# A decoder on one core: lane 7 of the batch-axis attention laid by GpSimd and lane 6 by ScalarE, where DMAs brought both

## The reference

```python
def split_heads(x):
    return x.reshape(L, N, h, d).transpose(1, 2, 0, 3)
q = split_heads(query @ q_proj.T + q_bias) * scale
k = split_heads(query @ k_proj.T + k_bias)
v = split_heads(query @ v_proj.T + v_bias)
scores = jnp.einsum('nhld,nhkd->nhlk', q, k)
scores = jnp.where(causal, scores, jnp.float32(-10000.0))
attn = jax.nn.softmax(scores, axis=-1)
ctx = jnp.einsum('nhlk,nhkd->nhld', attn, v)
ctx = ctx.transpose(2, 0, 1, 3).reshape(L, N, h * d)
return ctx @ out_proj.T + out_bias
```

## Time and profile before

| | us |
|---|---|
| median of 3 executions | 1265.68 |
| lowest, highest | 1263.89, 1273.03 |
| the profiled execution | 1265.68 |
| its span in the profile | 1263.9 |
| PE busy (share of the span) | 1133.7 (90%) |
| DVE busy | 908.6 (72%) |
| ACT busy | 565.4 (45%) |
| POOL busy | 261.0 (21%) |

### The profile page before, as it was taken

The page is one execution under the profiler, slowest core; times in us unless marked ns, Lnnn a source line. Parts: engine busy times, 40 slices in busy tenths (PEclk is TensorE's granted clock), DMA queues, the critical chain, the costliest instruction groups (busy, mean ns, idle before and its releaser), DMA issues. The chain is left out here.

```text
span 1263.9 us, 23937 instructions
## 1 busy us (share of the span) xinstructions
PE 1133.7 (90%) x8865; PEld 728.0 (58%) x8880; DVE 908.6 (72%) x2118; ACT 565.4 (45%) x1513; POOL 261.0 (21%) x338
## 2 busy tenths in 40 slices
PE   9799999899997999879898997779999999889975
PEld 3577888677763333335455555657777776344432
DVE  1799988589995878847988498854458778843325
ACT  4111112345433666746445243527777776232212
POOL 5000000022221111130542211130000000147752
PEclk9899989999998999999999999999999999989987
DMA  8011122300001242206000000229000000649556
GB/s 249 15 46 55 54 67 69 102 3 2 2 2 51 76 125 80 76 18 130 1 1 1 1 2 2 84 70 325 30 18 19 29 18 22 174 140 282 88 116 263
DMA packets 82847, 91.92 MB, mean 73 GB/s; under 512 B 25616, under 2 KB 66086, under 8 KB 82470
## 3 DMA queue, kind: packets, MB, share of 16 engines
q1 hardware_dynamic: 74332, 77.43, 20.5%
q0 software_dynamic: 6272, 9.25, 4.0%
q10 hardware_dynamic: 2128, 3.71, 0.8%
HBM read 68.00 MB, written 21.84 MB: 71 GB/s over the span
## 5 line engine op out<-in xcount | busy, mean ns | idle before, releaser
L401 DVE TENSOR_REDUCE gqa_x_slots<-gqa_scores 128x8 f32<-128x1024 f32 x64 | 78.4, 1226 | 29.4 <-PE gqa_scores L288 20.5
L1571 DVE TENSOR_REDUCE mla_neg_max<-mla_scores 128x8 f32<-128x1024 f32 x32 | 39.2, 1225 | 76.8 <-PE mla_scores L1436 51.3
L1518 ACT ACTIVATE mla_probs<-mla_scores,mla_neg_max 128x128 f32<-128x128 f32 x256 | 90.1, 388 | 0.0
L358 ACT ACTIVATE gqa_expT<-gqa_scoresT 128x1024 f32<-128x1024 f32 x64 | 65.5, 1023 | 48.2 <-PE gqa_scoresT L309 48.2
L309 PE MATMUL gqa_scoresT<-gqa_x_slotsT,gqa_keys 32*128 32x512 f32 x256 | 72.6, 639 | 10.4 <-issue 4.2
L2253 PE MATMUL ttt_z_ps<-ttt_prod,ident 128*128 128x256 f32 x288 | 70.1, 400 | 8.7 <-DVE ttt_prod L2329 8.7
L288 PE MATMUL gqa_scores<-gqa_keys_bd,xT 32*128 32x512 f32 x256 | 72.5, 663 | 2.7 <-DVE gqa_x_slots L401 1.4
L2253 PEld LDWEIGHTS ttt_z_ps<-ttt_prod,ident 128*128 128x128 f32 x288 | 54.8, 198 | 21.7 <-DVE ttt_prod L2329 14.6
L1426 PE MATMUL mla_q_ps<-xT,mla_merged_home 128*128 128x128 f32 x512 | 64.3, 280 | 1.6 <-PEq L63 1.6
L2260 PE MATMUL ttt_w_ps<-ttt_prod,ttt_neg_ident 128*128 128x144 f32 x448 | 59.2, 292 | 5.0 <-DVE ttt_prod L2362 5.0
L1426 PEld LDWEIGHTS mla_q_ps<-xT,mla_merged_home 128*128 128x128 f32 x512 | 61.2, 196 | 2.0 <-issue 1.8
(11 more groups left out here) (461 smaller groups left out, 2708.6 us busy)
## 6 DMA issues: line engine op xcount, KB each, us to landing
moe_w_gu<-in_moe_w_gu SPq DMA_DIRECT2D x24, 384.0 KB, 5.2
gqa_keys_bd<-in_gqa_keys_bd SPq DMA_DIRECT2D x16, 512.0 KB, 3.3
moe_w_dn<-in_moe_w_down SPq DMA_DIRECT2D x24, 192.0 KB, 5.8
moe_sums<-moe_zeros SPq DMA_DIRECT2D x2, 2176.0 KB, 11.7
xT<-in_x_feat SPq DMA_DIRECT2D x4, 512.0 KB, 7.4
ttt_k_by_head<-ttt_k_feat SPq DMA_DIRECT2D x8, 256.0 KB, 4.5
ttt_k_seq<-ttt_k_by_head SPq DMA_DIRECT2D x4, 512.0 KB, 5.2
x_tok<-in_mla_woT SPq DMA_DIRECT2D x8, 256.0 KB, 3.2
```

Source lines behind the costliest of these rows:

```text
L358: nc.scalar.activation(expT[:, k % 2, 2 * u:2 * u + 2, :], scoresT[:], ACT.Exp, scale=HD ** -0.5).then_inc(exp_ready, 1)
L401: nc.vector.tensor_reduce(x_slots[:, b % 2, :, c * NJ + 2 * half:c * NJ + 2 * half + 2, HD].rearrange("p g j -> p j g"), scores[:, of].rea ...
L1518: ins = nc.scalar.activation(probs[:, k % NB, e, i, :], scores[:, k % 2, e, i, :], ACT.Exp, bias=neg_max[:, k % 2, e, i:i + 1], accum_out= ...
```

## The change

Lanes 6 and 7 no longer come by DMA. ACT writes lanes 4 to 6, three instructions a strip. POOL writes lane 7, with a tensor_scalar of 128x512 a strip (`turned` times the mask's column), after the last turned block is kept and, from strip 3 on, after strip s - 3 is weighed. The DMAs, their semaphores and POOL's memsets of the lane blocks are gone. PE waits for POOL's semaphore in place of the DMAs'. On DVE, `divide(PAIRS - 2)` moves ahead of `shift(PAIRS - 1)`.

```diff
-        lane, BY_DVE, BY_DMA = inputs.lane, 4, 2
+        lane, BY_DVE = inputs.lane, 4
...
         @block.sync
         def _(sp):
-            sp.wait_ge(turn_kept, PAIRS)
-            for s in range(STRIPS):
-                sp.wait_ge(lanes_clear, min(s + 1, EB))
-                need(sp, weighed, s - EB + 1)
-                for r in range(R - BY_DMA, R):
-                    sp.dma_start(by_lane[s % EB][r::R, r], turned[r::R, s]).then_inc(lanes_loaded[s % EB], 16)
             sp.wait_ge(weighed, STRIPS - 1)
             fetch(sp, latent.merged_loads, merged)

         @block.gpsimd
         def _(pool):
             nc.gpsimd.memset(values[:, :, :, 1, :], 0.0).then_inc(pads_clear, 1)
-            nc.gpsimd.memset(by_lane[0][:, R - BY_DMA:R], 0.0).then_inc(lanes_clear, 1)
             for i in range(TAILED):
...
-            for n in range(1, EB):
-                pool.wait_ge(summed, 4 * PAIRS - 2 * (EB - 1 - n))
-                nc.gpsimd.memset(by_lane[n][:, R - BY_DMA:R], 0.0).then_inc(lanes_clear, 1)
+            pool.wait_ge(turn_kept, PAIRS)
+            for s in range(STRIPS):
+                need(pool, weighed, s - EB + 1)
+                nc.gpsimd.tensor_scalar(lane_of(s, R - 1), turned[:, s].rearrange("p x l -> p (x l)"), lane[:, R - 1:R], None, ALU.mult).then_inc(pool_laid, 1)
             for n in range(L):
                 norms[n % 2].gpsimd(pool, n // 2)
...
-                pe.wait_ge(lanes_loaded[n], 16 * BY_DMA * (s // EB + 1))
+                pe.wait_ge(pool_laid, s + 1)
...
-                for r in range(BY_DVE, R - BY_DMA):
+                for r in range(BY_DVE, R - 1):
                     ins = nc.scalar.mul(lane_of(s, r), turned[:, s].rearrange("p x l -> p (x l)"), lane[:, r:r + 1])
...
+            divide(PAIRS - 2)
             shift(PAIRS - 1)
-            divide(PAIRS - 2)
             divide(PAIRS - 1)
```

More of the change, by code:

```diff
@@ L875, in batch_axis_attention @@
         turn_ready, turn_kept, weighed, att_kept = sem("turn_ready"), sem("turn_kept"), sem("weighed"), sem("att_kept")
-        dve_laid, act_laid, lanes_clear = sem("dve_laid"), sem("act_laid"), sem("lanes_clear")
-        lanes_loaded = [sem(f"lanes_loaded{n}") for n in range(EB)]
+        dve_laid, act_laid, pool_laid = sem("dve_laid"), sem("act_laid"), sem("pool_laid")
         out_ready, chain, merged = sem("out_ready"), sem("chain"), sem("merged")
```

## The result

| | before | changed |
|---|---|---|
| median time, us | 1267.39 (20 runs, 1263.89 to 1276.46) | 1276.97 (20 runs, 1273.23 to 1287.39) |
| profiled execution: time, span, us | 1265.68, 1263.9 | 1279.03, 1277.2 |
| weighing stage, first lane on DVE to start of the output projection on PE, us | 788.33 to 809.01: 20.68 | 789.02 to 817.73: 28.71 |

The ratio of the times is 1.0081, 95% interval [1.006, 1.0101]: slower, by 0.6 to 1.0%, or 7.6 to 12.8 us of 1267.39. The forecast was 1269.0 with a range of 1265.0 to 1275.5, so the median lies 1.5 us above the range. In the forecast the stage grew by 3.3 us; in the trace it grows by 28.71 - 20.68 = 8.03 us, which is 0.63% of 1267.39 and within the interval.

A forecast was written before the change was run, and what follows sets the result against it. DVE was taken to bound the weighing stage. ACT's third lane and POOL's eight holds of DVE each led to about 809.3, together one loss of 3.3 us: 1265.68 + 3.3 = 1269.0 us, range 1265.0 to 1275.5.

The forecast's parts named there:

- The bottleneck of before: Weighing stage: DVE bounds it, starting one four-lane instruction every 2.21 us without a pause, the last ending at 806.04.
- SP's DMAs and the memsets gone, worth 0: Weighing stage: dropping SP's 16 lane DMAs and POOL's memsets of lanes 6 and 7 changes nothing, 0 us.
- ACT's third lane, +3.3: Weighing stage: ACT's eight extra lane instructions end at 809.15, so PE's last strip starts 3.3 us later.
- 0.41 us of DVE per lane on POOL: Weighing stage: each POOL lane keeps DVE off the shared SBUF port 0.41 us, eight times, ending DVE at 809.3.
- POOL itself is not late: a lane is some 0.60 us by the copy row: Weighing stage: POOL's lane takes 0.60 us, priced from a 256-element copy of 397 ns, or about 2.9 behind DVE.
- The configuration instruction, worth 0: Ahead of POOL's first lane: an added configuration instruction takes 0.1 us at about 783.4, early enough to cost 0.
- The reorder, worth 0 with 0.3 us of cover: DVE ahead of the stage: divide(6) before shift(7) costs 0, with 0.3 us to spare before PE's last turn.
- The bound of +8.8: Weighing stage: upper bound of the loss, from POOL holding DVE 1.1 us a lane, by a 1300 ns two-operand product.
- (a): Weighing stage: POOL's tensor_scalar holds DVE longer than a copy; +6.4 at 0.8 us, +8.8 at 1.1; chance 0.30.
- (b): Weighing stage: POOL can't get between DVE's back-to-back instructions and waits until DVE stops after three strips; +8 us; chance 0.07.
- (c): POOL's first lane: code behind the configuration instruction must load, past its cover up to 3 us late; chance 0.06.
- (d): Elsewhere than in the weighing stage: the change wins by over 1%; chance 0.03.

The follow-up runs named there:

- e3: Changed kernel with POOL's lane 7 as a plain copy, without the mask multiplication; ratio to the kernel before 1.0064 [1.0027, 1.0102].
- e5: Changed kernel with POOL multiplying lane 7 by the constant 1.5 instead of the mask's column; timed once, 1292.45 us against 1272.32 for the kernel before.
- e9: Kernel before with DVE's lanes as one tensor_scalar each, and strip 0's lanes 4 and 5 moved from ACT to DVE; ratio 0.9976 [0.9947, 1.0006].
- e1: Kernel before with only lane 6 moved from DMA to ACT, lane 7 still by DMA; ratio 0.9997 [0.9969, 1.0024].
- e4: Changed kernel with DVE's four lanes as four tensor_scalar, one tensor input each, instead of one two-input instruction; ratio to the kernel before 1.0011 [0.9969, 1.0054].
- e2: Kernel before with only lane 7 moved from DMA to POOL, lane 6 still by DMA; ratio 1.0082 [1.0045, 1.0118].
- e11: Kernel before with only divide(6) moved ahead of shift(7) on DVE; timed once, no ratio, stage 20.67 us against 20.68.
- e6: Changed kernel with POOL's lane 7 as a tensor_tensor, the mask's column broadcast as second tensor input; ratio to the kernel before 1.0078 [1.004, 1.0116].
- e10: Changed kernel with DVE's four-lane instruction cut into four two-input instructions of 128x512; ratio to the kernel before 1.0055 [1.0014, 1.0097].
- e7: Changed kernel with five unread matmuls added to keep PE busy ahead of strip 0; ratio to the kernel before 1.0094 [1.0052, 1.0135].

## Why the prediction was wrong

Laid one on the other, three of these kernels give the 8.03 us as a ladder; each rung adds to the one below:

| kernel | stage, us | step | what comes in |
|---|---|---|---|
| before | 20.68 | | |
| e3, a copy | 24.42 | +3.74 | the hold of 0.41, ACT's third lane, PE's half clock in strip 0 |
| e5, a constant | 25.30 | +0.88 | the operation: it ends 1.37 instead of 0.48 behind DVE's instruction |
| changed, a column | 28.71 | +3.41 | a second wait for DVE, where DVE has more queued |

The forecast had the first rung, 3.3 for 3.74 (two holds too many, the wait and POOL's 0.48 missing), and nothing of the other two. The last rung is POOL's chain: its eight lanes run without a gap in both kernels, for 22.07 us with the constant and 25.47 with the column, 3.40 more. By records: two are a DVE period longer (5.78 against 3.59, 4.84 against 2.64: 4.39), two that start in DVE's pauses are 1.1 shorter each (1.56 against 2.64), and the other four together 1.1 longer. The rungs are differences of single profiles; the times can't tell them apart.

By the prediction's steps:

- **The bottleneck of before**, DVE at 2.21 us a strip: right. In e9, where DVE is faster, PE no longer waits for it at the last strip, but most of e9's gain is the earlier first strip.
- **SP's DMAs and the memsets gone, worth 0**: nothing speaks against it, though no run takes them away by themselves. With and without the DMAs of lane 6 the stage is 28.86 and 28.71, but POOL bounds it in both.
- **ACT's third lane, +3.3**: right in the trace (e1, 3.30), but in the changed kernel covered by POOL. What it left out is that PE's longer idleness ahead of strip 0 drops its clock; the later start and the slower strip make DVE wait for strip 0's buffer: 0.52 us in e3, where it counts, and 1.36 in e1, where it costs nothing because ACT is later still.
- **0.41 us of DVE per lane on POOL**: right in size for a copy and for this tensor_scalar. It isn't paid eight times, though: six times in e3 and three times, 1.05 us in all, in the changed kernel, where DVE is often idle.
- **"POOL itself is not late: a lane is some 0.60 us by the copy row ... up to about 2.9 where it waits for a running DVE instruction of 2.28 first"**: this is the step that failed, and with it the sum. A lane is 1.56 us alone, not 0.60, and with more queued on DVE it waits for two of DVE's instructions, not for one: 5.78 and 4.84 us against the 2.9. POOL's chain of 25.5 us became the longest. The ladder weighs the two errors: the longer lane 0.88 us, the second wait 3.41. The rows of before had copies and products on POOL and none with a column, so none showed a second wait. The first error was to give one price to two quantities. The copy row was a fair proxy for how long POOL *holds* the shared port, since both move 512 elements. It was no proxy for how long the *instruction lasts*, which has the operation in it and one more read. The bounds were only set for the hold, and the duration, which had no row in the trace at all, was taken at the low end without any. The product of two operands, 1300 ns in the earlier trace rows, stood in the text as a bound of the hold; as a price of the duration it was the nearer one.
- **The configuration instruction, worth 0**: right. It ran at 782.6 (not 783.4, since the change itself brings divide(6) forward), and the first lane of e4 is no longer than the others. In e2 POOL is idle for only 4.2 us ahead of its first lane, which takes the same 5.78 as in the changed kernel behind 6.4 us.
- **The reorder, worth 0 with 0.3 us of cover**: right (e11).
- **The sum on 1265.68**: the median of 20 runs of the kernel before is 1267.39. The bound of +8.8 stood at 1274.5 on the single run; on this median it is 1276.2. The stage's 8.03 us on this median is 1275.4, inside the range. That is luck: the 8.8 of the bound was for DVE held 1.1 us a lane, and DVE isn't held by that. What the mechanism of the forecast gives is 3.3 us, and the measured loss is 7.6 to 12.8.

The rivals: (a) a longer hold: not in the change, the hold stayed 0.41, though true of two tensor inputs (e6). (b) POOL shut out until DVE pauses: half a truth, and its +8 us is the measured 8.03 by chance. POOL is passed over by one queued instruction of DVE, not by all (e10), and the pauses of DVE after three strips that were named as its sign came about in another way, through late POOL lanes. (c) loading: no cost at the first lane (e4). (d) a win: none. The sign that was to show the forecast wrong, POOL named as PE's releaser, is there in each long wait.

What is argued and not shown is that the second wait is the read of the *column*. Shown is that it comes with the pointer to the column and goes with the constant (e5), and that it shrinks with the length of DVE's instruction (e10). A kernel with the column elsewhere than in SBUF wasn't tried.

## What to carry to other kernels

When work goes to an engine that shares a port, price two things from two rows: how long it keeps the neighbour out, and how long its own instruction lasts with all its waits; then ask for each engine, the helper too, whether its own chain is the longest. Where a neighbour runs long two-input instructions back to back, a per-partition scalar read by pointer on POOL can cost an entire further instruction of the neighbour (2.2 us here); a constant, or shorter instructions on the neighbour (4 x 128x512 for 128x2048: 3.1 us off the stage), brings most of that back. Ahead of moving lanes, look at the form of the bounding instruction: the same four lanes as tensor_scalar took DVE 1.67 us instead of 2.28 (e9). And where an engine has no row of the form that it is to run, set bounds on its own duration too, not only on what it takes from its neighbour.

## What the runs showed of the hardware

- POOL's tensor_scalar of 128x512 with a column takes 1.56 us alone, and holds a two-input DVE instruction for 0.41 us; with two tensor inputs it holds it for 0.84 (e6). So the hold isn't as long as the instruction; that it goes by the elements POOL reads is the simplest reading of the three forms.
- Beside queued two-input DVE instructions of 2.28 us it waits twice (5.78 and 4.84 us), with a constant once (2.6 to 3.6 us), a copy once (2.67 to 2.74 us). The Trainium skill ("SBUF — State Buffer", section SBUF: two separate sides) has the shared pair as an exclusive lock that whoever starts first keeps for the whole instruction. For POOL's wait the copies agree: they end 0.48 us behind DVE's instruction. For DVE's wait they don't: it is held 0.41 us by a POOL instruction that runs on for 1.36 us from the moment DVE's ends, so POOL doesn't keep it out for the whole instruction. That one POOL instruction may have to get past two DVE instructions follows from no sentence there.
- DVE's tensor_scalar of 128x512 has records of 0.48 us with POOL silent and starts every 0.40 (e9); four take 1.66 us, and 2.46 beside a POOL lane (e4).
- PE stayed at a granted clock of 1.00 in strip 0 after 1.9 us of idleness (before), and had 0.56 there after 2.5 (e3) and 0.50 after 3.9 (changed), for 1.96, 3.35 and 3.64 us. The idle time alone doesn't decide: in e7 strip 3, behind three strips at full clock and 2.56 us of idleness, had 1.00 and took 2.05 us; in the changed kernel strip 4, behind 2.89 us, had 0.58 and took 3.27.
